# Loops kept on the engines instead of written out, in a two-layer attention and expert kernel

## The chip, the cores and the metric

The kernel runs on one core of one Trainium2 chip. The metric is the device time of one execution in microseconds (us). Three executions of the kernel before took 1290.54, 1291.73 and 1295.01 us, a median of 1291.73 us.

A core has five instruction streams that run beside each other and meet only in semaphores: PE (TensorE, matmuls; a page lists its weight loads as PEld), DVE (VectorE), ACT (ScalarE), POOL (GpSimd) and SP (SyncE, which here only issues DMAs). Each stream is read by a sequencer, which waits for semaphores, works on registers, branches, and hands the other instructions to its engine.

## The reference

Input are tokens x (4 batches, 512 tokens, 256 values), a context of the same shape and a mask. Four blocks follow, each added to x; 16 heads of width 16 throughout. Cut to what matters:

```python
x = x + xattn0(layernorm(x), ctx, ctx, mask)   # masked cross attention
x = x + ffn0(layernorm(x))                     # self attention, then 8 experts (256->1024->256), one per token
x = x + xattn1(layernorm(x), ctx, ctx)         # cross attention with biases
x = x + ffn1(layernorm(x))                     # softmax gate of width 256, 8 experts (256->256), one per token

# attention, for every batch and head
scores = q @ k.T / sqrt(16); weights = softmax(scores); out = (weights @ v) @ W_O
# experts
idx = argmax(gate(x)); y = relu(x @ w1[e] + b1[e]) @ w2[e] + b2[e] for e = idx
```

## The kernel before

The program has five stages of one shape, called in this order on every engine: attention `xa0` (masked), attention `sa0`, experts `me0`, attention `xa1`, experts `me1`. Every engine has a stream of its own, written in the order in which it runs; there is no scheduler. Semaphores carry counts that only grow: `Signal.at(i, k)` gives the count `i * per + lead + k` to wait for in round i.

**Projection** (`project_vector`, `project_gpsimd`, `project_scalar`, `project_tensor`, `project_sync`). Per batch: layer norm statistics on DVE (L423, L426), the reciprocal root on POOL (L529, L531), the normalised tokens on DVE (L435), transposes and q, k, v matmuls on PE (L643, L651, L668, L681), q and k split into three bfloat16 parts (ACT L598 and L603, DVE L454, POOL L536), and the parts stored in HBM by SP (L729). `each_batch` (DVE, POOL) goes over batches 0 to 2 and then does batch 3 apart; `each_pair` (PE, ACT) does batches 0 and 1, then 2 and 3 apart.

**Attention** (`attend_*`). A batch has 4 groups of 4 heads, a group has 16 units of 128 x 512 scores. PE computes, for every unit, transposed scores (L994, with a mask matmul L998 in `xa0`), and the plain scores of a unit 28 ahead (L981), of which DVE takes row maxima (L372 in `xa0`, L376 elsewhere). ACT exponentiates (L908). After every fourth unit PE multiplies by the values (L1008, four float32 matmuls). Three PSUM banks each go round for the two kinds of scores, so PE can be at most three units ahead of ACT and of DVE. SP brings the rows of a group from HBM two groups ahead (`load_stacks`, L334) and puts 12 rows of maxima beside them (L815). `body(b, first, last)` is one batch: it is called for batch 0, for batches 1 and 2 in a loop, and for batch 3.

**Experts** (`gate_*`, `route_*`, `expert_*`, `combine_*`). Tokens are gated (DVE L1336 to L1349), sorted into 23 slots of 128 rows, gathered by POOL (L1595), multiplied slot by slot on PE (L1730, L1738, L1755 in `me0`, L1749 in `me1`, transposes L1721), finished by DVE (L1694) and stored. The expert of a slot is known at run time only: it is loaded into a register, and addresses are worked out from it, so the kernel before has register instructions in these stages. `each_slot` does slots 0 to 5, then two rounds of 6 in a loop, then the last 5.

In the kernel before all of these loops are Python's: each iteration is written into the stream, and every wait compares with a constant.

Of the kernel before, what the change touches and what calls it, by code (L numbers as in the profile page):

```python
# [38 lines left out]
T = S // P  # L39
# [20 lines left out]
class Signal:  # L60
# [6 lines left out]
    def at(self, i, k=0):  # L67

        return i * self.per + (self.lead + k)


# [148 lines left out]
class Attention:  # L220


    def __init__(self, nc, stage, mem, dram, name, w, cross, norms, affine, cols, rows, masked, self_block,
# [8 lines left out]
        def sig(what, per, lead=0):  # L232
            self.used.append(stage.enter_context(nc.semaphore(f"{name}_{what}")))
            return Signal(self.used[-1], per, lead)

        self.stat = [sig(f"stat{n}", T) for n in range(norms)]
        self.aggr = [sig(f"aggr{n}", T) for n in range(norms)]
# [56 lines left out]
def each_batch(eng, body):  # L294

    for b in range(B - 1):
        body(b, b + 1)
    body(B - 1, None)


def each_pair(eng, body):

    for i in range(B // 2 - 1):
        for odd in range(2):
            body(2 * i + odd, 2 * i + (odd + 1), odd)
    for odd in range(2):
        b = B - 2 + odd
        body(b, b + 1 if b + 1 < B else None, odd)
# [56 lines left out]
def maximum(dve, a, G, v, bank):  # L365

    mem = a.mem
    h, t = v // T, v % T
    out = mem.m[:, t, h:h + 1]
    if a.masked:  # L370
        dve.wait_ge(a.s_ps.sem, a.s_ps.at(G, v + 1))
        ins = dve.tensor_tensor_reduce(mem.junk[bank], mem.ps[:, bank, :], mem.mbS[:, t, :], 1.0, FLOOR,  # L372
                                       ALU.add, ALU.max, out)
    else:
        dve.wait_ge(a.s_ps.sem, a.s_ps.at(G, v + 1))
        ins = dve.tensor_reduce(out, mem.ps[:, bank, :], AX.X, ALU.max)  # L376
    ins.then_inc(a.s_max.sem, 1)
# [15 lines left out]
def project_vector(dve, a):  # L393
# [16 lines left out]
    def normalise_first(b):  # L410
        dve.wait_ge(a.scale[0].sem, a.scale[0].at(b, 2))
        if type(b) is not int or b:
            dve.wait_ge(a.hT_ps.sem, a.hT_ps.at(b))
        for t in range(T):
            dve.tensor_scalar(mem.hn[:, t, :], mem.x[:, b, t, :], mem.mv_in[:, b, t, 0:1], mem.rstd_in[:, b, t:t + 1],
                              ALU.subtract, ALU.mult).then_inc(a.first_norm.sem, 1)

    def statistics(b):
        for t in range(T):
            if a.norms == 2:  # L420
                dve.wait_ge(a.first_norm.sem, a.first_norm.at(b, t + 1))
            src = mem.x[:, b, t, :] if a.norms == 1 else mem.hn[:, t, :]
            dve.bn_stats(mem.stats[:, t, :], src).then_inc(a.stat[last].sem, 1)  # L423
        for t in range(T):
            dve.wait_ge(a.stat[last].sem, a.stat[last].at(b, t + 1))
            dve.bn_aggr(mem.mv[:, t, :], mem.stats[:, t, :]).then_inc(a.aggr[last].sem, 1)  # L426

    def normalise(b):

        dve.wait_ge(a.scale[last].sem, a.scale[last].at(b, 2))  # L430
        if a.norms == 1 and (type(b) is not int or b):
# [83 lines left out]
def project_gpsimd(pool, a):  # L515
# [192 lines left out]
def project_sync(sp, a):  # L708
# [98 lines left out]
def attend_sync(sp, a, meanwhile, then=None):  # L807
# [39 lines left out]
    body(0, True, False)  # L847
    for b in range(1, B - 1):
        body(b, False, False)
# [7 lines left out]
def last_sums(eng, a, name, b, k):  # L857
# [13 lines left out]
    eng.tensor_tensor(mem.total_x[:, two, :], x, u, ALU.add).then_inc(a.acc_ready.sem, 1)  # L871
    eng.wait_ge(a.acc_ready.sem, a.acc_ready.at(b, k + 1))
    eng.tensor_copy(x, u).then_inc(a.x_done.sem, 1)


def attend_gpsimd(pool, a):
    mem = a.mem

    def gather(b, g):

        G = NG * b + g
        if not (type(b) is int and G < 2):
            pool.wait_ge(a.pv.sem, a.pv.at(G - 1))
        pool.tensor_copy(mem.vg[g % 2][:, :, :, 0:DK],  # L884
# [5 lines left out]
    for g in range(NG):  # L890
        gather(0, g)
    for b in range(1, B):
        for g in range(NG):
# [5 lines left out]
def attend_scalar(act, a, meanwhile):  # L899
# [56 lines left out]
    body(0, True, False)  # L956
    for b in range(1, B - 1):
        body(b, False, False)
# [7 lines left out]
def attend_tensor(pe, a, meanwhile):  # L966
# [154 lines left out]
    body(0, True, False)  # L1121
    for b in range(1, B - 1):
        body(b, False, False)
# [12 lines left out]
def attend_vector(dve, a, meanwhile, beside=None):  # L1136
# [33 lines left out]
    def block_input(b, k):  # L1170

        u, row = mem.block_in[:, 2 * k:2 * k + 2, :], mem.rows[:, a.rows + 1:a.rows + 2, :].to_broadcast([P, 2, D])
        if type(b) is not int or b:
            dve.wait_ge(a.x_done.sem, a.x_done.at(b - 1, k + 1))
        for t in range(2 * k, 2 * k + 2):
# [45 lines left out]
    body(0, True, False)  # L1221
    for b in range(1, B - 1):
        body(b, False, False)
# [21 lines left out]
class Mixture:  # L1245
# [5 lines left out]
    def __init__(self, nc, stage, mem, dram, name, affine, gate_width, row, hidden, b2, weights, loads,  # L1251
                 x_done, space, acc_stored, gathered, earlier, scattered=None, fetched=None, out_stored=None):
        self.mem, self.dram, self.name, self.affine = mem, dram, name, affine
# [5 lines left out]
        def sig(what, per, lead=0):  # L1259
            self.used.append(stage.enter_context(nc.semaphore(f"{name}_{what}")))  # L1260
            return Signal(self.used[-1], per, lead)

        self.stat = sig("stat", T)
# [40 lines left out]
        if hidden is None:  # L1304
            self.out_stored = Signal(out_stored, 16)


def gate_vector(dve, m):
# [20 lines left out]
    def body(b):  # L1329
# [18 lines left out]
        dve.wait_ge(m.choice.sem, m.choice.at(b, CHOICE - 1))  # L1348
        dve.tensor_copy(mem.expert[:, b, :], mem.expert_u[:, :]).then_inc(m.choice.sem, 1)  # L1349
# [17 lines left out]
    def rest_of_batches():  # L1367
# [3 lines left out]
        for b in range(early, B):  # L1371
            normalise(b)
        for b in range(1, B):
            body(b)
# [213 lines left out]
def expert_gpsimd(pool, m, done=()):  # L1588
# [14 lines left out]
    for stage in done:  # L1603
        for sem in stage.used:
            pool.sem_clear(sem)
# [252 lines left out]
def program(nc, x, ctx_in, mask, wa, wb, wc, cols, rows, b1c, b2, gate0, w1, w2, gate1, we, be, out):  # L1858
# [10 lines left out]
    with ExitStack() as ctx:  # L1869
        mem = Memory(nc, ctx)  # L1870
        def semaphore(name):
            return ctx.enter_context(nc.semaphore(name))

        x_first, x_rest, weights_a, weights_qo, loaded, setup, acc_stored, out_stored = (semaphore(n) for n in (
            "x_first", "x_rest", "weights_a", "weights_qo", "loaded", "setup", "acc_stored", "out_stored"))
        weights = [semaphore(f"weights{i}") for i in range(2)]
# [63 lines left out]
        with ExitStack() as again:  # L1940
# [10 lines left out]
        me1 = Mixture(nc, ctx, mem, dram, "me1", None, D, 4, None, mem.be, (weights[1], 16 * (C * E + NG)), (),  # L1951
                      xa1.x_done, None, None, gathered, 1, fetched=fetched, out_stored=out_stored)

# [159 lines left out]
```

## Time and profile before

| what | value |
|---|---|
| the profiled execution | 1290.54 us |
| its span, first to last instruction | 1288.8 us |
| PE busy | 1142.8 us (89%) |
| DVE, ACT, POOL busy | 851.6, 669.7, 225.5 us |
| mean granted clock of TensorE | 0.945 of full |
| instructions fetched (queues named instruction) | 49 packets of 16 KB, 42 of 8 KB |

The profile shows one execution. Busy time counts an engine's instructions from start to end; register, branch and semaphore instructions are not in it. A row of idle time names the work that ended it. TensorE's clock is granted at one of two levels, 2.4 GHz (1.00) or 1.2 GHz (0.50); a number between them is a mean over a stretch. Time is from the first instruction.

### The profile page before, as it was taken

How to read it: one execution, taken by the hardware profiler on the slowest of the kernel's cores; microseconds unless marked ns; L12 is line 12 of the kernel's file. 1: busy time of each engine (PE TensorE's matmuls, PEld its weight loads, DVE VectorE, ACT ScalarE, POOL GpSimd, SP SyncE). 2: the span in 40 equal slices, each digit the busy share in tenths (PEclk: the TensorE clock that was granted, in tenths of full speed). 3: DMA queues.
4: the chain of work that ended last, by engine and by line, in shares of the span. 5: the costliest groups of instructions: out<-in, count | busy, mean ns of one | idle time of the engine just before them, and what ended most of it. 6: DMA issues, size and time to landing. Idle time of an engine off the chain costs nothing. (4 is left out here: it accounts for less than half of the span.)

```text
span 1288.8 us, 17972 instructions
## 1 busy us (share of the span) xinstructions
PE 1142.8 (89%) x5757; PEld 551.3 (43%) x5786; DVE 851.6 (66%) x2112; ACT 669.7 (52%) x1357; POOL 225.5 (17%) x280
## 2 busy tenths in 40 slices
PE   7989999999988999999968999994989999998490
PEld 4523343433354223333364666663532343335370
DVE  5787777777468888888771222224788888876722
ACT  2446666666633577677712333331536777675350
POOL 5310000000134000000202222213420000101054
PEclk9979999999999899999968999998989999999785
DMA  6943232321038443543291140103773422211064
GB/s 213 314 137 106 79 83 50 84 50 26 1 117 287 122 105 84 130 101 92 71 371 37 31 156 31 32 5 99 249 249 76 103 59 75 71 34 58 25 165 145
DMA packets 103371, 139.32 MB, mean 108 GB/s; under 512 B 8044, under 2 KB 86320, under 8 KB 101872
## 3 DMA queue, kind: packets, MB, share of 16 engines
q1 hardware_dynamic: 99200, 127.94, 33.0%
q0 software_dynamic: 4080, 10.23, 3.0%
q8 instruction: 49, 0.80, 0.3%
q14 instruction: 42, 0.34, 0.1%
HBM read 86.30 MB, written 52.17 MB: 107 GB/s over the span
## 5 line engine op out<-in xcount | busy, mean ns | idle before, releaser
L908 ACT ACTIVATE r<-ps 128x512 f32<-128x512 f32 x768 | 427.7, 599 | 213.0 <-PE ps L994 123.6
L376 DVE TENSOR_REDUCE m<-ps 128x1 f32<-128x512 f32 x512 | 321.1, 683 | 46.9 <-PE ps L981 46.6
L981 PE MATMUL ps<-r 96*128 96x512 bf16 x720 | 281.9, 394 | 20.5 <-DVE m L376 7.0
L994 PE MATMUL ps<-r 99*128 99x512 bf16 x768 | 294.2, 388 | 5.6 <-ACT r L908 5.6
L372 DVE CUSTOM_DVE_ANT_0 r<-ps,r 128x512 bf16<-128x512 f32 x256 | 170.2, 690 | 60.0 <-PE ps L981 59.5
L1008 PE MATMUL ps<-r 128*32 128x512 f32 x1536 | 205.4, 607 | 4.9 <-ACT r L908 3.3
L994 PEld LDWEIGHTS ps<-r 99*128 99x128 bf16 x768 | 74.4, 98 | 212.2 <-ACT r L908 157.4
L981 PEld LDWEIGHTS ps<-r 96*128 96x128 bf16 x720 | 71.3, 99 | 106.8 <-DVE m L376 24.7
L884 POOL COPY r<-r 128x256 f32<-128x256 f32 x48 | 19.0, 399 | 543.6 <-PE ps L1008 543.6
L681 PE MATMUL ps<-r,w 128*128 128x512 f32 x192 | 91.7, 611 | 0.0
L1683 DVE COPY r<-ps 128x512 f32<-128x512 f32 x46 | 31.8, 692 | 90.5 <-PE ps L1730 90.5
L1642 ACT ACTIVATE r<-ps,cols 128x128 f32<-128x128 f32 x46 | 18.6, 454 | 137.7 <-PE ps L1721 137.7
L1730 PE MATMUL ps<-r 128*128 x184 | 86.2, 612 | 2.7 <-issue 0.4
L998 PE MATMUL ps<-r,identb 128*128 128x512 bf16 x227 | 87.2, 384 | 0.0
L1755 PE MATMUL ps<-r 128*128 x368 | 83.3, 379 | 1.1 <-ACT r L1652 1.1
L1694 DVE TENSOR_TENSOR r<-ps,r 128x256 f32<-128x256 f32 x46 | 19.5, 424 | 97.2 <-PE ps L1755 68.8
L598 ACT ACTIVATE r<-ps,cols 128x512 bf16<-128x512 f32 x48 | 32.9, 686 | 94.2 <-PE ps L681 94.2
L1755 PEld LDWEIGHTS ps<-r 128*128 128x128 f32 x368 | 69.8, 190 | 20.2 <-issue 11.9
L536 POOL TENSOR_TENSOR r<-r 128x512 bf16<-128x512 f32 x48 | 55.0, 1163 | 65.6 <-ACT r L603 65.6
L1008 PEld LDWEIGHTS ps<-r 128*32 128x32 f32 x1536 | 30.3, 108 | 84.3 <-ACT r L908 66.6
L1595 POOL DMA_INDIRECT r<-token_rows,source x46 | 44.5, 968 | 69.1 <-DVE source L1534 31.8
L1652 ACT ACTIVATE r<-ps,b1c 128x128 f32<-128x128 f32 x184 | 50.1, 383 | 11.3 <-PE ps L1738 11.2
(155 smaller groups left out, 1274.5 us busy)
## 6 DMA issues: line engine op xcount, KB each, us to landing
r<-q_parts SPq DMA_DIRECT2D x48, 384.0 KB, 5.1
r<-k_parts SPq DMA_DIRECT2D x48, 384.0 KB, 5.9
k_parts<-r SPq DMA_DIRECT2D x24, 384.0 KB, 3.1
q_parts<-r SPq DMA_DIRECT2D x24, 384.0 KB, 3.1
r<-in_w SPq DMA_DIRECT2D x16, 512.0 KB, 4.8
r<-in_w SPq DMA_DIRECT2D x8, 1024.0 KB, 14.5
k_parts<-r SPq DMA_DIRECT2D x24, 256.0 KB, 3.2
q_parts<-r SPq DMA_DIRECT2D x24, 256.0 KB, 3.1
```

What stands on the lines that cost most here:

```text
L372: ins = dve.tensor_tensor_reduce(mem.junk[bank], mem.ps[:, bank, :], mem.mbS[:, t, :], 1.0, FLOOR, ALU.add, ALU.max, out)
L376: ins = dve.tensor_reduce(out, mem.ps[:, bank, :], AX.X, ALU.max)
L536: pool.tensor_tensor(mem.parts[n][:, 2, :], mem.res[n % 2], mem.parts[n][:, 1, :], ALU.subtract).then_inc(a.lo.sem, 1)
L681: ins = pe.matmul(ps[:, QK_BANK + n, :], a.w[:, 0 if of_query(n) else 1, c, (n % C) * P:(n % C + 1) * P], src[:, c, :], start=(c == 0), st ...
L908: act.activation(mem.probs[:, u // HG, u % HG, :], ps[:, ST + (UNITS * g + u) % DEEP, :], ACT.Exp, scale=SCALE).then_inc(a.p_exp.sem, 1)
L981: pe.matmul(ps[:, led_bank(n), :], mem.qst[g][0:ROWS, h, t * P:(t + 1) * P], mem.kst[g][0:ROWS, h, :], start=True, stop=True).then_inc(a.s ...
L994: ins = pe.matmul(out, mem.kst[g][0:KROWS, h, kt * P:(kt + 1) * P], mem.qst[g][0:KROWS, h, :], start=True, stop=not a.masked)
L998: ins = pe.matmul(out, mem.identb[:, :], mem.mbT[:, batch, kt, :].rearrange("p b n -> p (b n)"), start=False, stop=True)
L1008: ins = pe.matmul(ps[h * VW:(h + 1) * VW, OB, :], mem.vg[g % 2][:, kt, h, :], mem.probs[:, kt, h, :], start=(kt == 0), stop=(kt == T - 1))
L1652: ins = act.activation(mem.midT[:, f, :], ps[:, TM[f // 4], (f % 4) * P:(f % 4 + 1) * P], ACT.Relu, bias=mem.b1c[:, bass.ds(e * FT + f, 1)])
L1730: ins = pe.matmul(ps[:, UP[k], :], mem.xT[j % 2][:, c, :], w, start=(c == 0), stop=(c == C - 1))
L1755: ins = pe.matmul(ps[:, DOWN[j % 2], 0:D], mem.midT[:, f, :], w, start=(f == 0), stop=(f == FT - 1))
```

## The change

Seven loops are now loops of the engine that runs them: `Fori(first, end)` emits the body once, sets a register, and ends the body with an addition and a conditional branch back. All five engines have them. The batch number b in the body is then a register. A wait for `Signal.at(b, k)` compares with a register that has to be worked out first, and an address that holds b (of x, v, the mask, rows in HBM) too. Some instructions take no wait on a register; for these `wait_alone` emits a semaphore instruction of its own, which holds the wait and counts up a semaphore that nobody reads. It is written in at ten places, whether b is a register there or not. The semaphore for stored outputs is now made by the stage that uses it, and POOL clears the three new semaphores of the first two stages.

```diff
+def wait_alone(eng, sem, value, passed):
+
+    eng.wait_ge(sem, value)
+    eng.sem_inc(passed, 1)
@@ each_batch
-    for b in range(B - 1):
+    with eng.Fori(0, B - 1) as b:
         body(b, b + 1)
@@ each_pair
-    for i in range(B // 2 - 1):
+    with eng.Fori(0, B // 2 - 1) as i:
@@ maximum, masked
-        dve.wait_ge(a.s_ps.sem, a.s_ps.at(G, v + 1))
+        wait_alone(dve, a.s_ps.sem, a.s_ps.at(G, v + 1), a.passed["dve"])
@@ statistics, normalise
-            dve.wait_ge(a.stat[last].sem, a.stat[last].at(b, t + 1))
+            wait_alone(dve, a.stat[last].sem, a.stat[last].at(b, t + 1), a.passed["dve"])
-        dve.wait_ge(a.scale[last].sem, a.scale[last].at(b, 2))
+        wait_alone(dve, a.scale[last].sem, a.scale[last].at(b, 2), a.passed["dve"])
@@ project_gpsimd
-        pool.wait_ge(a.aggr[last].sem, a.aggr[last].at(b, T))
+        wait_alone(pool, a.aggr[last].sem, a.aggr[last].at(b, T), a.passed["pool"])
@@ project_sync
-        for b in range(0, B - 2):
+        with sp.Fori(0, B - 2) as b:
@@ attend_sync, attend_scalar, attend_tensor, attend_vector: the same in each
-    for b in range(1, B - 1):
+    with sp.Fori(1, B - 1) as b:
         body(b, False, False)
@@ attend_gpsimd
-    for b in range(1, B):
+    with pool.Fori(1, B) as b:
@@ gate_vector
-            dve.wait_ge(m.logit.sem, m.logit.at(b, t // 2 + 1))
+            wait_alone(dve, m.logit.sem, m.logit.at(b, t // 2 + 1), m.passed["dve"])
-            dve.wait_ge(m.choice.sem, m.choice.at(b, t + 1))
+            wait_alone(dve, m.choice.sem, m.choice.at(b, t + 1), m.passed["dve"])
-        for b in range(1, B):
+        with dve.Fori(1, B) as b:
             body(b)
@@ each_slot
-    for i in range(1, rounds):
+    with eng.Fori(1, rounds) as i:
         for j in range(DEPTH):
             body(i * DEPTH + j, j, i)
```

No work on the engines changes its order. What moves is what stands between. First PE, in a group of `sa0`, batch 1: before, around the transposes of the maxima and the first products that follow.

```order
L994 MATMUL ps<-r 128x512
L981 MATMUL ps<-r 128x512
L1016 MATMUL ps<-identb,mparts 12x128 x4
L994 MATMUL ps<-r 128x512
L981 MATMUL ps<-r 128x512
L1008 MATMUL ps<-r 32x512 x4
```

The same place now (L996 and L1002 are the old L994, L989 the old L981, L1024 the old L1016, L1016 the old L1008; an ISA row without a tile is several register operations in one instruction):

```order
L996 REGISTER_ALU
L1002 MATMUL ps<-r 128x512
L988 REGISTER_ALU
L989 MATMUL ps<-r 128x512
L1021 ISA
L1024 MATMUL ps<-identb,mparts 12x128 x4
L996 REGISTER_ALU
L1002 MATMUL ps<-r 128x512
L988 REGISTER_ALU
L989 MATMUL ps<-r 128x512
L1011 REGISTER_ALU
L1016 MATMUL ps<-r 32x512 x4
```

Each of the two matmuls of a unit has a register instruction ahead of it, and so has each set of transposes or products. In the whole loop body of PE these are 157 instructions in `xa0` and 150 in `sa0` and `xa1`, where the body has some 1000 and 832 instructions with weight loads and both passes of float32 matmuls counted.

Second DVE, in the projection of `xa0`, one batch of the loop. Before:

```order
L454 SCALAR_TENSOR_TENSOR r<-ps,cols,r 128x512
L423 BN_STATS stats<-x 128x6 x4
L426 BN_AGGR mv<-stats 128x2 x4
L454 SCALAR_TENSOR_TENSOR r<-ps,cols,r 128x512
L435 TENSOR_SCALAR r<-x,mv,rstd 128x256 x4
```

Now, from the last statistics on (L431 is the old L423, L434 the old L426, L462 the old L454, L443 the old L435). The semaphore instructions of `wait_alone` are not printed in this listing; one stands ahead of each BN_AGGR and ahead of the first L443:

```order
L431 BN_STATS stats<-x 128x6
L74 ISA
L434 BN_AGGR mv<-stats 128x2
L74 REGISTER_ALU
L434 BN_AGGR mv<-stats 128x2
L74 REGISTER_ALU
L434 BN_AGGR mv<-stats 128x2
L460 REGISTER_ALU
L461 REGISTER_ALU
L462 SCALAR_TENSOR_TENSOR r<-ps,cols,r 128x512
L74 ISA
L443 TENSOR_SCALAR r<-x,mv,rstd 128x256 x4
```

Four aggregations that stood in a row are now three instructions each: a register instruction, a semaphore instruction and the aggregation. The DVE body of a batch has 22 or 23 register instructions, and 28 to 30 with semaphore and branch instructions.

## Rows read from the trace of the kernel before

**Rows 1.** The page: busy time, share of the span and instructions.

```profile
PE 1142.8 (89%) x5757; PEld 551.3 (43%) x5786; DVE 851.6 (66%) x2112; ACT 669.7 (52%) x1357; POOL 225.5 (17%) x280
```

**Rows 2.** Windows: length, busy time (instructions) per engine, granted clock, DMA share, GB/s.

```profile
88.00:370.00 282.00, 274.43 (x1528) 110.99 (x1555) 200.82 (x650) 173.33 (x305) 13.67 (x27) 1.00 0.21 55
441.00:656.00 215.00, 203.77 (x1196) 78.75 (x1195) 183.35 (x413) 149.14 (x282) 21.57 (x34) 1.00 0.42 113
...
893.00:968.00 75.00, 61.19 (x208) 31.75 (x208) 62.84 (x115) 30.30 (x52) 29.47 (x32) 0.84 0.66 214
968.00:1182.00 214.00, 206.98 (x1204) 75.10 (x1204) 173.21 (x369) 152.24 (x292) 16.95 (x26) 1.00 0.26 67
...
1226.00:1258.00 32.00, 29.47 (x134) 22.93 (x134) 9.76 (x23) 16.52 (x44) 17.82 (x19) 0.90 0.62 169
```

**Rows 3.** Waits, whole span: who waited for whom, us, times, longest.

```profile
PEld ps L981 <- DMA r<-k_parts: 10.0, 13, 1.6
PE ps L1721 <- DMA r<-token_rows,source: 10.2, 4, 4.8
```

**Rows 4.** Timeline of PE in `xa1`: start, length, instruction, idle before.

```profile
1072.67 0.39 PE L994 MATMUL ps<-r 99*128 99x512 bf16 x1
1072.90 0.38 PE L981 MATMUL ps<-r 96*128 96x512 bf16 x1
1073.12 0.38 PE L994 MATMUL ps<-r 99*128 99x512 bf16 x1
```

**Rows 5.** Timeline of PE: the routing matmuls of `me0`.

```profile
675.76 1.11 PE L1556 MATMUL ps<-r 128*128 128x69 bf16 x16 [6.88 <-DVE r L1522]
```

**Rows 6.** Chain that ended last, in `me1`: start, us, what (DVEq is DVE's sequencer).

```profile
1237.88 0.07 DVEq L1694
1237.96 0.05 issue
...
1243.54 0.22 PE ps L1721 x2
1243.76 0.87 PE ps L1749 x4
```

**Rows 7.** DMA queues: packets, MB, share of 16 engines; issues: KB, us to landing.

```profile
q8 instruction: 49, 0.80, 0.3%
q14 instruction: 42, 0.34, 0.1%
...
cols<-in_cols SPq DMA_DIRECT2D x1, 10.0 KB, 1.8
```

**Rows 8.** Chain that ended last, in the projection of `xa1`.

```profile
905.45 0.29 DVE mv L426 x3
905.74 0.08 issue
905.82 0.24 POOL var L529
906.05 0.07 issue
906.13 1.05 POOL rstd L531
```

**Rows 9.** Chain that ended last, in the gate of `me1`.

```profile
1193.43 0.18 DVE expert_u L1347
1193.63 0.04 DVE expert L1349
```

**Rows 10.** Timeline of the weight loads in `sa0`, batch 1: waits for a stack.

```profile
537.60 0.10 PEld L981 LDWEIGHTS ps<-r 96*128 96x128 bf16 x1 [0.45 <-DMA r<-k_parts]
550.33 0.10 PEld L981 LDWEIGHTS ps<-r 96*128 96x128 bf16 x1 [0.18 <-DMA r<-k_parts]
564.62 0.10 PEld L981 LDWEIGHTS ps<-r 96*128 96x128 bf16 x1 [0.99 <-DMA r<-k_parts]
```

**Rows 11.** Windows around a fall of the clock, columns as in rows 2.

```profile
60.00:80.00 20.00, 15.07 (x56) 5.81 (x54) 19.04 (x53) 7.46 (x11) 5.26 (x6) 0.89 0.74 266
80.00:100.00 20.00, 19.13 (x78) 6.00 (x80) 14.28 (x47) 9.16 (x16) 0.00 (x0) 0.77 0.36 97
...
380.00:400.00 20.00, 16.91 (x62) 9.80 (x62) 14.17 (x33) 10.69 (x18) 8.71 (x9) 1.00 0.82 244
```

More of the change, by code:

```diff
@@ L234, in sig @@
             return Signal(self.used[-1], per, lead)
+        self.passed = {eng: stage.enter_context(nc.semaphore(f"{name}_{eng}_passed")) for eng in ("dve", "pool")}
         self.stat = [sig(f"stat{n}", T) for n in range(norms)]
@@ L410, in normalise_first @@
     def normalise_first(b):
-        dve.wait_ge(a.scale[0].sem, a.scale[0].at(b, 2))
+        wait_alone(dve, a.scale[0].sem, a.scale[0].at(b, 2), a.passed["dve"])
         if type(b) is not int or b:
@@ L871, in last_sums @@
     eng.tensor_tensor(mem.total_x[:, two, :], x, u, ALU.add).then_inc(a.acc_ready.sem, 1)
-    eng.wait_ge(a.acc_ready.sem, a.acc_ready.at(b, k + 1))
+    wait_alone(eng, a.acc_ready.sem, a.acc_ready.at(b, k + 1), a.passed[name])
     eng.tensor_copy(x, u).then_inc(a.x_done.sem, 1)
@@ L882, in gather @@
         if not (type(b) is int and G < 2):
-            pool.wait_ge(a.pv.sem, a.pv.at(G - 1))
+            wait_alone(pool, a.pv.sem, a.pv.at(G - 1), a.passed["pool"])
         pool.tensor_copy(mem.vg[g % 2][:, :, :, 0:DK],
@@ L956, in attend_scalar @@
     body(0, True, False)
-    for b in range(1, B - 1):
+    with act.Fori(1, B - 1) as b:
         body(b, False, False)
@@ L1121, in attend_tensor @@
     body(0, True, False)
-    for b in range(1, B - 1):
+    with pe.Fori(1, B - 1) as b:
         body(b, False, False)
@@ L1173, in block_input @@
         if type(b) is not int or b:
-            dve.wait_ge(a.x_done.sem, a.x_done.at(b - 1, k + 1))
+            wait_alone(dve, a.x_done.sem, a.x_done.at(b - 1, k + 1), a.passed["dve"])
         for t in range(2 * k, 2 * k + 2):
@@ L1221, in attend_vector @@
     body(0, True, False)
-    for b in range(1, B - 1):
+    with dve.Fori(1, B - 1) as b:
         body(b, False, False)
@@ L1251, in __init__ @@
     def __init__(self, nc, stage, mem, dram, name, affine, gate_width, row, hidden, b2, weights, loads,
-                 x_done, space, acc_stored, gathered, earlier, scattered=None, fetched=None, out_stored=None):
+                 x_done, space, acc_stored, gathered, earlier, scattered=None, fetched=None):
         self.mem, self.dram, self.name, self.affine = mem, dram, name, affine
@@ L1261, in sig @@
             return Signal(self.used[-1], per, lead)
+        self.passed = {eng: stage.enter_context(nc.semaphore(f"{name}_{eng}_passed")) for eng in ("dve",)}
         self.stat = sig("stat", T)
@@ L1304, in __init__ @@
         if hidden is None:
-            self.out_stored = Signal(out_stored, 16)
+            self.out_stored = sig("out_stored", 16)
 def gate_vector(dve, m):
@@ L1347, in body @@
         dve.tensor_scalar(mem.expert_u[:, :], mem.idx8[:, :, 0], E - 1, None, ALU.bitwise_and).then_inc(m.choice.sem, 1)
-        dve.wait_ge(m.choice.sem, m.choice.at(b, CHOICE - 1))
+        wait_alone(dve, m.choice.sem, m.choice.at(b, CHOICE - 1), m.passed["dve"])
         dve.tensor_copy(mem.expert[:, b, :], mem.expert_u[:, :]).then_inc(m.choice.sem, 1)
@@ L1603, in expert_gpsimd @@
     for stage in done:
-        for sem in stage.used:
+        for sem in (*stage.used, *stage.passed.values()):
             pool.sem_clear(sem)
@@ L1872, in semaphore @@
             return ctx.enter_context(nc.semaphore(name))
-        x_first, x_rest, weights_a, weights_qo, loaded, setup, acc_stored, out_stored = (semaphore(n) for n in (
-            "x_first", "x_rest", "weights_a", "weights_qo", "loaded", "setup", "acc_stored", "out_stored"))
+        x_first, x_rest, weights_a, weights_qo, loaded, setup, acc_stored = (semaphore(n) for n in (
+            "x_first", "x_rest", "weights_a", "weights_qo", "loaded", "setup", "acc_stored"))
         weights = [semaphore(f"weights{i}") for i in range(2)]
@@ L1951, in program @@
         me1 = Mixture(nc, ctx, mem, dram, "me1", None, D, 4, None, mem.be, (weights[1], 16 * (C * E + NG)), (),
-                      xa1.x_done, None, None, gathered, 1, fetched=fetched, out_stored=out_stored)
+                      xa1.x_done, None, None, gathered, 1, fetched=fetched)
         with nc.Block() as block:
```

## The prediction

> **What bounds the kernel now.** I read the page's busy line first: PE is busy 89% of the span, the next engine 66% [rows 1]. Then windows cut at the stages. In the three attention loops PE is busy 274.43 of 282, 203.77 of 215 and 206.98 of 214 us at clock 1.00, 685.18 of 711 us together, 55% of the span; the projection of `xa1` has 61.19 of 75 us with DVE at 62.84 [rows 2]. So two kinds of stretch have to be told apart. In attention an added instruction costs nothing while PE's sequencer stays ahead of its engine, and a stop of PE costs its whole length. In projection and gate DVE and POOL are links of the chain of waits [rows 8, 9], and instructions between short operations count.
>
> The change takes no engine work away and adds none. Every term is a sequencer's: register instructions, semaphore instructions, branches, and the fetching of instructions after a branch back.
>
> **What a register instruction costs.** The nearest row: in `me1` the chain passes DVE's sequencer, where such an instruction takes 0.07 us and 0.05 us pass before the operation behind it starts [rows 6]. So 0.07 us where instructions queue, up to 0.12 us where one stands between a wait and its operation. For PE there is a bound. A slot of `me1` takes 0.22 + 0.87 = 1.09 us, just its matmuls at full rate [rows 6], although its stream already has about 8 register, load and wait instructions beside 16 weight loads and matmuls. Sixteen pairs of load and matmul of 69 columns go by in 1.11 us, 0.069 us a pair at most [rows 5]. So the 8 take at most (1.09 - 8 x 0.069) / 8 = 0.067 us each.
>
> **Attention bodies: 0.** A unit of `sa0` or `xa1` has two matmuls, 0.23 and 0.22 us apart [rows 4]: 0.45 us. Its sequencer work after the change is 2 x 0.069 for the pairs and 2 x 0.07 for the registers, 0.28 us; with 0.12 us a register it is 0.38 us. Both stay under 0.45 us, and `xa0` has a third matmul per unit. ACT and DVE have one register instruction per 0.6 us operation. What hides the cost is PE's own matmul time; without it the 157 + 2 x 150 register instructions of PE's bodies, run twice, would be 914 x 0.07 = 64 us, which is the far end.
>
> **Branches back in attention: 7.2.** Each body runs twice, so each engine goes back once per attention. After a branch the instructions have to be there. They are streamed: PE's packets are 0.80 MB / 49 = 16 KB, 256 instructions, the others' 8 KB, 128 instructions [rows 7]. PE's bodies are 1000, 832 and 832 instructions, 3.9, 3.3 and 3.3 packets. If the start of the body is gone, PE stands until it has come again. The queue's 0.3% of 16 engines' 1288.8 us over 49 packets is 1.26 us a packet, and the smallest load has a landing time of 1.8 us for 10 KB [rows 7]: at most 1.8 + 1.3 = 3.1 us, at least the 0.12 us of the branch if the start is still there. I take 2.4 us, nearer to the fetch. ACT, DVE and SP go back at the same unit, and their stops lie beside PE's, so one stop counts per loop: 3 x 2.4 = 7.2 us (0.4 to 9.3).
>
> By the Trainium skill (Runtime: NRT & Kernel Launch, Instruction fetch mechanics) a taken branch whose target is not among the two pages held forces a fetch before execution goes on, and prefetch runs forward only; by that rule all three branches stop PE, as in the term taken. The same section gives PE room for 2048 instructions; a body of 1000 would fit, and if all of that room counted the term would fall to its low end, 0.4 us. It gives 16 KiB for every engine's block, where this trace has 8 KB for the others.
>
> **Branches back over slots: 3.6.** One per engine in `me0` and in `me1`. PE's body in `me0` is 669 instructions, 2.6 packets, in a stretch that PE bounds: 2.4 us. In `me1` (151 instructions) the gathers leave PE waiting at times [rows 3], so half, 1.2 us. Bounds 0.2 and 6.2 us.
>
> **Projection: 4.5.** `each_batch` runs its body three times in each of three stages, nine in all. The chain goes from statistics through aggregations (three in 0.29 us, 0.10 us each) to POOL and the root [rows 8], then to the tokens and PE. An aggregation is now three instructions of the sequencer, at least 0.21 us: four of them add 0.5 us, the wait on its own ahead of POOL's first operation and of the tokens 0.12 us each, POOL's register instructions and the addresses of the statistics the rest: 1.0 us. Nine times 1.0 is the top. These stretches are partly held by DMAs (share 0.66 on average, and 0.82 in one stretch with POOL and DVE half free [rows 2, 11]), which such a delay lies beside. I take half, 4.5 us (1 to 9).
>
> **Gate: 2.7.** Three looped batches in each of two stages. Five operations in a row depend on the one before; two of them are 0.20 us apart and 0.17 us long [rows 9]. Each gets a register instruction or a wait of its own: 5 x 0.09 = 0.45 us, six times 2.7 us (1 to 4).
>
> **SP: 2.0.** Per group four or five register instructions come in ahead of the loads, 0.5 us. In `sa0`, batch 1, the score matmuls already wait for their stack by 0.45, 0.18 and 0.99 us [rows 10], so the room there is nil and 4 x 0.5 = 2.0 us go through. Elsewhere PE waits 13 times in the whole span, mostly in batch 0 [rows 3], which isn't looped. No row shows a load whose HBM address is a register; if it costs SP nothing more the term is 2.0, and at another 0.5 us for each of two loads in 8 groups it is 10.
>
> **Small branches: 1.5.** About ten that lie on the chain, of DVE in projection and gate, with bodies of 34 to 54 instructions, which I take to be still at hand: 0.15 us each. If half of them found theirs gone it would be 5 x 1.8 = 9.
>
> **The sum.** 0 + 7.2 + 3.6 + 4.5 + 2.7 + 2.0 + 1.5 = 21.5 us. On the profiled execution, 1290.54 us (span 1288.8), that is 1312.0 us; the median of the runs shown is 1.2 us above it, so 1313 us. The cases at the low ends of all terms give 0.4 + 0.2 + 1 + 1 + 2 + 0.5 = 5 us.
>
> **Rivals.** *Nothing is refetched, 1300 us.* The bodies are still there at every branch back, and only the register instructions of projection, gate and SP remain: 4.5 + 2.7 + 2.0 + ten branches at 0.15, less than 11 us with the range, 1298 to 1303. For it speaks that 3.9 packets are little, against it that the fetches are as many as the stream has packets [rows 7], one after another, with nothing that shows a store of old ones.
>
> *The clock falls more often, 1330 us.* TensorE was at 1.00 over 20 us in which PE was busy 16.91 us, and went down to half behind a stretch with 15.07 of 20 [rows 11]. A projection whose batches are a microsecond longer has a lower share. One more period of half clock per projection, as long as the one whose mark is the mean 0.77 (9 of 20 us and what lies before it, some 14 us), costs up to half its length, 7 us; three are 20 us. [...]
>
> *PE's sequencer becomes the bound in attention, 1340 us.* If a wait against a register costs 0.15 us more than one against a constant, a unit needs 0.58 us instead of 0.45 in `sa0` and `xa1`; two looped batches of 64 units in each are 256 x 0.13 = 33 us, less what products (1 us per four units) win back. The bound of 0.067 us above speaks against it, but that stretch waits against constants.
>
> *Not slower, 1292 us.* The place is the projection. If each of them is held by its DMAs and not by DVE, its nine delays vanish, SP's vanish where a stack has room, and with the bodies still at hand the whole change is what is left of the gate, about 1 to 3 us. It decides at a term under 4 us in all. DMA shares of 0.66 to 0.82 speak for it, the chain through DVE and POOL [rows 8] against it. A gain would need a fetch that is saved; PE's idle time in attention is only 26 of 711 us [rows 2], mostly waits for others, so a gain over 4 us has next to no room.
>
> **How the numbers follow.** The measurement can tell about 0.3%, 3.9 us, from no change. Forecast (1303 to 1324): 0.56. Nothing refetched (1296 to 1303): 0.16. Clock or sequencer (above 1324): 0.16. Not slower: 0.12, of which faster 0.03. So faster 0.03, same 0.09, slower 0.88. The range for 8 in 10 leaves out the not-slower case and the far half of the slow ones: 1296 to 1335 us. The likeliest case alone has 1303 to 1324.
>
> **What would show it.** In the profile after: near the middle of each attention PE should have one gap of 2 to 3 us that ends in "issue", and the instruction queues more packets than 49 and 42. PE's matmuls in a looped batch should be as far apart as in a written one (0.22 us). The projections should be 1 to 3 us longer, with aggregations 0.2 us apart; the waits for k_parts in `sa0`, batch 1, longer by half a microsecond. The forecast is wrong if the packets stay at 91 without gaps (then the first rival), if the looped batches are longer throughout (the third), or if the mean clock falls below 0.93 (the second).

## The result, and the profile after

The changed kernel took 1304.7 us (median of 4, 1301.71 to 1306.56), the kernel before 1292.44 us (1290.54 to 1295.01) beside it. The ratio is 1.0079, 95% interval 1.0056 to 1.0101: slower by 10.2 us (7 to 13). A second set gave 1.0083 (1.0067 to 1.0099), 10.7 us. I had forecast 1313 us, +21.3: the direction was right, the size twice what came, and the time lies in the lower part of the range.

The profiled execution spans 1303.4 us from first to last instruction, 14.6 us more than the 1288.8 before, so some 4 us of what this one profile shows are not in the difference of the runs. First the page: busy times as in [rows 1], and the queues that bring instructions, as in [rows 7].

```profile
PE 1144.9 (88%) x5786; PEld 550.4 (42%) x5787; DVE 855.6 (66%) x2113; ACT 669.1 (51%) x1358; POOL 225.5 (17%) x280
...
q8 instruction: 40, 0.66, 0.2%
q14 instruction: 46, 0.38, 0.1%
```

The engines are as busy as before, within 4 us each; the whole growth is time between instructions. PE fetched 9 packets fewer, the others 4 more. The records hold 12524 different instructions of PE before and 10281 now (an iteration counted once), 48.9 and 40.2 packets of 256, and 49 and 40 were fetched: PE fetched nothing twice. That alone speaks against my largest term. The others hold 5372 different instructions, 42.0 packets of 128, and fetched 46: some of theirs came twice.

Windows over the same stretches as in [rows 2], shifted by as much as PE's stream had moved (length, busy time of PE, PEld, DVE, ACT, POOL, clock, DMA share, GB/s):

```profile
88.00:370.00 282.00, 275.57 (x1552) 110.36 (x1551) 200.69 (x649) 171.45 (x302) 13.34 (x26) 1.00 0.21 55
445.00:660.00 215.00, 202.80 (x1192) 78.75 (x1193) 182.27 (x410) 147.51 (x280) 21.46 (x33) 1.00 0.41 113
...
900.00:976.00 76.00, 60.28 (x208) 31.44 (x208) 62.59 (x113) 30.17 (x52) 29.36 (x32) 0.86 0.65 211
976.00:1190.00 214.00, 206.82 (x1208) 75.92 (x1208) 174.63 (x372) 152.19 (x292) 16.94 (x26) 1.00 0.26 68
```

In attention PE's busy time per window is within 1.2 us of before. The waits as in [rows 3]: those for a stack are shorter than before, not longer.

```profile
PE ps L1731 <- DMA r<-token_rows,source: 10.1, 3, 4.9
PEld ps L989 <- DMA r<-k_parts: 7.5, 8, 1.4
```

The timeline of PE at the place of [rows 4] (start, length, instruction). The matmuls of a looped batch are 0.22 us apart, as written out:

```profile
1072.67 0.39 PE L1002 MATMUL ps<-r 99*128 99x512 bf16 x1
1072.89 0.38 PE L989 MATMUL ps<-r 96*128 96x512 bf16 x1
1073.11 0.38 PE L1002 MATMUL ps<-r 99*128 99x512 bf16 x1
```

And PE where it goes back in `sa0` (the branch is at 536.0). I had put a stop of 2.4 us of PE here; there is none:

```profile
535.27 0.38 PE L989 MATMUL ps<-r 96*128 96x512 bf16 x1
535.58 1.06 PE L1016 MATMUL ps<-r 128*32 128x512 f32 x8
536.58 0.39 PE L1002 MATMUL ps<-r 99*128 99x512 bf16 x1
536.80 0.38 PE L989 MATMUL ps<-r 96*128 96x512 bf16 x1
```

One engine does stop. DVE goes back in `xa0` at 219.26, and the first instruction of its body comes 2.86 us later, with two packets for the smaller streams (at 220.3 and 222.8) meanwhile. Its timeline there:

```profile
219.12 0.69 DVE L380 CUSTOM_DVE_ANT_0 r<-ps,r 128x512 bf16<-128x512 f32 x1
219.73 0.08 DVE L380 DVE_READ_ACCUMULATOR2_ANT m<- 128x1 f32 x1
222.42 0.69 DVE L380 CUSTOM_DVE_ANT_0 r<-ps,r 128x512 bf16<-128x512 f32 x1 [2.60 <-issue]
```

PE was far enough ahead: its matmuls at 222 are 0.22 us apart, and between 220 and 240 it loses 0.1 us against before.

To see where the 10 us are I took the time between the same two weight loads of PE in each trace (they come in the same order). What grew, in us, in two profiles of the changed kernel (the second is e5's):

| stretch | before | after, first | after, second |
|---|---|---|---|
| projection of `sa0` | 58.2 | +2.05 | +2.02 |
| projection of `xa1` | 71.3 | +1.44 | +0.72 |
| looped batches of `xa0`, `sa0`, `xa1` | 137.8, 112.2, 108.9 | +0.31, +1.46, +0.20 | +0.28, +1.22, +0.19 |
| gate of `me0`, of `me1` | 16.8, 25.1 | +1.39, +1.52 | +1.81, +1.52 |
| looped slots of `me0`, of `me1` | 100.2, 17.6 | +1.23, +0.57 | +1.31, +0.14 |
| `me1`, slots 0 to 5 | 9.4 | +3.89 | -0.48 |

The growth sits in short chains: projection, gate, slots. The looped batches of attention, 359 us, add 2.0 and 1.7 us, nearly all of it in `sa0` (see e12).

### The profile page after: what moved, and what is told of

The parts are those of the page before. It is cut to its first block, busy times and chain, and to the rows that moved or that the text cites. A ratio compares the mean times of both kernels' runs of the same rounds, so it can differ in the third digit from the quotient of the medians.

```text
span 1303.4 us, 21372 instructions
## 1 busy us (share of the span) xinstructions
PE 1144.9 (88%) x5786; PEld 550.4 (42%) x5787; DVE 855.6 (66%) x2113; ACT 669.1 (51%) x1358; POOL 225.5 (17%) x280
## 4 chain that ended last, share of the span: by engine, by line
PE 67%; DVE 12%; DMA 7%; issue 6%; ACT 4%; POOL 2%; SPq 1%; DVEq 1%; POOLq 0%; ACTq 0%
PE ps L1016 12%; PE ps L1002 11%; PE ps L989 9%; PE ps L1740 7%; PE ps L1765 6%; DMA r<-k_parts 5%; PE ps L1006 4%; PE ps L1067 3%; DVE m L384 2%; PE ps L676 2%; PE ps L1759 2%; ACT r L916 2%; PE ps L689 2%; PE ps L1748 1%; DVE r L443 1%
## 5 line engine op out<-in xcount | busy, mean ns | idle before, releaser
L1002 PE MATMUL ps<-r 99*128 99x512 bf16 x768 | 293.9, 388 | 6.2 <-ACT r L916 6.2
L989 PE MATMUL ps<-r 96*128 96x512 bf16 x720 | 281.7, 393 | 19.1 <-DVE m L384 7.0
L1016 PE MATMUL ps<-r 128*32 128x512 f32 x1536 | 204.5, 604 | 5.5 <-ACT r L916 4.5
L1002 PEld LDWEIGHTS ps<-r 99*128 99x128 bf16 x768 | 74.4, 98 | 211.7 <-ACT r L916 152.2
L989 PEld LDWEIGHTS ps<-r 96*128 96x128 bf16 x720 | 71.2, 99 | 107.8 <-DVE m L384 24.2
L892 POOL COPY r<-r 128x256 f32 (+1 forms) x48 | 19.0, 400 | 543.7 <-PE ps L1016 543.7
L1006 PE MATMUL ps<-r,identb 128*128 128x512 bf16 (+1 forms) x256 | 98.2, 384 | 0.0
L1016 PEld LDWEIGHTS ps<-r 128*32 128x32 f32 x1536 | 30.3, 107 | 84.1 <-ACT r L916 63.0
## 6 DMA issues: line engine op xcount, KB each, us to landing
r<-in_w SPq DMA_DIRECT2D x8, 1024.0 KB, 14.6
```

What stands on the lines that cost most here:

```text
L989: pe.matmul(ps[:, led_bank(n), :], mem.qst[g][0:ROWS, h, t * P:(t + 1) * P], mem.kst[g][0:ROWS, h, :], start=True, stop=True).then_inc(a.s ...
L1002: ins = pe.matmul(out, mem.kst[g][0:KROWS, h, kt * P:(kt + 1) * P], mem.qst[g][0:KROWS, h, :], start=True, stop=not a.masked)
L1006: ins = pe.matmul(out, mem.identb[:, :], mem.mbT[:, batch, kt, :].rearrange("p b n -> p (b n)"), start=False, stop=True)
L1016: ins = pe.matmul(ps[h * VW:(h + 1) * VW, OB, :], mem.vg[g % 2][:, kt, h, :], mem.probs[:, kt, h, :], start=(kt == 0), stop=(kt == T - 1))
```

## The experiments

Theory A, formed from this: the branches back are free, because PE still holds the body; what costs is the loops' register instructions and, once e1 had run, any instruction put between a wait and its operation. Its rival is my prediction's: refetching.

### Attention loops alone: e2 and e7

Of the changed kernel only the attention loops stay; in e7 `wait_alone` also leaves out its counting instruction where the value is a constant, so that the operation itself waits, as before.

```diff
 # each_batch, each_pair, project_sync, gate, each_slot:
-    with eng.Fori(0, B - 1) as b:
+    for b in range(0, B - 1):
 # e7 alone, wait_alone:
     eng.wait_ge(sem, value)
-    eng.sem_inc(passed, 1)
+    if type(value) is not int:
+        eng.sem_inc(passed, 1)
```

> Only the loops of the three attentions are loops of the engines (all five engines); projection, gate and slots are written out. The traces show PE's stream 0.6 us later at the end of xa0, level through xa1, and no fetch of PE for 80 us in the second iteration. Theory A (PE holds its body, nothing is refetched): 1293 to 1296 us, 1 to 3 us over before. Rival, that each of the three branches back stops PE for 2.4 us as I had predicted: 1299 to 1301 us.

> Only the attention loops are loops of the engines, and a separate wait is written only where its value is a register; everywhere else the operation waits itself, as in the kernel before. Theory A (attention is free, as PE holds its body): 1290 to 1293 us, within 0.2% of before. Rival (a branch back costs 2.4 us each): 1297 us.

e2: 1297.37 us, ratio 1.0071 (1.0044 to 1.0098), but its runs scatter over 11 us. e7: 1290.03 against 1290.78 us, ratio 0.9993 (0.9982 to 1.0004), with 42 packets for PE instead of 49. So the attention loops alone cost at most 0.5 us; e2 contains the separate waits besides, which turned out to be a cost (e1).

One thing differs between the two. DVE's body in `xa0` has 325 instructions in all of these kernels. In e2 and in both profiles of the changed kernel it was not held: from the branch to the next instruction 2.88, 2.86 and 2.83 us. In e7 it was, 0.35 us, and the others' packets are 42 there against 50 in e2. The body stands at another place in DVE's stream (it begins near instruction 330 in e7, 399 and 436 in the changed kernel and e2); that the place decides is not shown. So e7 does not contain this stop. What it costs is small: `xa0`'s looped batches are 0.1 us longer in the changed kernel than in e7, and up to 0.9 us longer in e2.

### How long a body PE holds: e13, e14, e9a, e9b

As e7, with counting instructions put into the looped body of `sa0` on PE: 9, 13, 17 and 26 per unit in e13, e14, e9a and e9b. They change no data. Each of these kernels ran once.

```diff
             for u in range(UNITS):
+                for _ in range(17 if a.name == "sa0" and not first and not last else 0):
+                    pe.sem_inc(a.passed["pe"], 1)
                 transposed_scores(b, g, u, first)
```

> As e7 (only the attention loops looped, waits joined), with 17 counting instructions more per unit on PE in the looped body of sa0: 832 + 64 x 17 = 1920 instructions, 7.5 packets of 16 KB. They change no data. Theory A (PE holds what it has run, up to 2048 instructions, as the Trainium skill has it: Runtime: NRT & Kernel Launch, Instruction fetch mechanics): the second iteration fetches nothing, and PE goes back within 0.3 us. Theory B (what is held is about the 1000 instructions seen so far): 7 or 8 packets again in the second iteration, and one stop of 1 to 3 us at the branch back. In both the two looped batches are longer by 2 x 64 x (17 x 0.05 us - what a unit's matmuls hide): some 50 to 70 us in all.

> The same with 26 instructions per unit: 832 + 64 x 26 = 2496 instructions, 9.75 packets. Theory A (room for 2048): the start is gone at the branch back, the second iteration fetches its 9 or 10 packets again and PE stops there once, for a packet's 1 to 3 us, the price that my prediction put on each branch back. Theory C (the room is larger): no fetch in the second iteration and no stop.

> As e9a with 9 counting instructions per unit: a body of 832 + 576 = 1408 instructions, 5.5 packets. A body of 1000 was held, one of 1920 not. If the room is 2048 less what is fetched ahead of need, this one is held: no stop at the branch back (under 0.4 us) and no fetches for most of the second iteration. If the room is about 1024: a stop of 3.5 us and 6 more packets.

> The same with 13 per unit: 832 + 832 = 1664 instructions, 6.5 packets. Held or not closes the gap between 1408 and 1920; with a room of 2048 and one packet ahead it is held, with half of that not.

The recorded body of `sa0` has 784 instructions, 48 fewer than the 832 that I had counted (and `xa0`'s about 955, not 1000); the table has the recorded numbers.

| kernel | body | PE's packets | from the branch to PE's next instruction | time |
|---|---|---|---|---|
| e7 | 784 | 42 | 0.29 us | 1290 us |
| e13 | 1360 | 44 | 0.28 us | 1396 us |
| e14 | 1616 | 45 | 0.28 us | 1478 us |
| e9a | 1872 | 55 | 3.70 us | 1554 us |
| e9b | 2448 | 61 | 3.48 us | 1737 us |

The added instructions themselves are 2.3, 3.3, 4.3 and 6.5 packets. So e13 and e14 have what the longer text explains (44, 45), and e9a has 9 more than the 46 it explains: it fetched its body of 7.3 packets again. e9b, with a body of 9.6, has 12 to 13 more. Why both are 2 or 3 above their body is not shown. PE around the branch in e9a, timeline; the idle time before the first matmul of the units beside it is 1.8 to 1.9 us, at the branch 5.75:

```profile
661.04 0.61 PE L1003 MATMUL ps<-r 99*128 99x512 bf16 x1 [1.81 <-issue]
661.44 0.63 PE L990 MATMUL ps<-r 96*128 96x512 bf16 x1
667.82 0.61 PE L1003 MATMUL ps<-r 99*128 99x512 bf16 x1 [5.75 <-issue]
668.22 0.63 PE L990 MATMUL ps<-r 96*128 96x512 bf16 x1
670.77 0.60 PE L1003 MATMUL ps<-r 99*128 99x512 bf16 x1 [1.92 <-issue]
```

The same place in e14, body still held (the first row shown is the unit before the branch, the third the one after it):

```profile
623.52 0.39 PE L1003 MATMUL ps<-r 99*128 99x512 bf16 x1 [0.63 <-ACT r L917]
623.74 0.38 PE L990 MATMUL ps<-r 96*128 96x512 bf16 x1
626.27 0.61 PE L1003 MATMUL ps<-r 99*128 99x512 bf16 x1 [2.15 <-issue]
626.67 0.63 PE L990 MATMUL ps<-r 96*128 96x512 bf16 x1
628.49 0.61 PE L1003 MATMUL ps<-r 99*128 99x512 bf16 x1 [1.19 <-ACT r L917]
```

So a refetch costs PE more than I had priced: 3.5 to 3.7 us, above my upper bound of 3.1. It isn't paid up to 1616 instructions. By the Trainium skill (Runtime: NRT & Kernel Launch, Instruction fetch mechanics) PE has room for 2048 instructions; 1616 held and 1872 not agrees with that room less a block of 256 that is already being filled ahead, which is an estimate of mine. The same section's two-page window, by which all these bodies would be refetched, doesn't hold for PE here. The expectation of "50 to 70 us" for the added work was far off; see the last section.

### The separate waits: e1 and e6

e1 is the changed kernel with all loops written out: only `wait_alone` is left of the change, at eleven places (three of them, in attention, are not in the shortened diff above). e6 is the same, with its two instructions in the other order, so that the count goes first and the operation itself waits.

```diff
 # e6, wait_alone:
-    eng.wait_ge(sem, value)
-    eng.sem_inc(passed, 1)
+    eng.sem_inc(passed, 1)
+    eng.wait_ge(sem, value)
```

> All loops are written out again, as in the kernel before; only the separate semaphore instructions of wait_alone are left. Theory A (what costs is the loops: their register instructions and what happens around branches): within 0.1% of the kernel before, 1291 to 1294 us, since a semaphore instruction takes 0.02 to 0.05 us in the trace and about 8 of them per batch of a projection or gate lie on the chain: 18 batches x at most 0.1 us = 2 us. Theory B (the separate waits are what makes projection and gate longer): 1297 us or more, half of the 12 us.

> As e1, all loops written out, but the counting instruction of wait_alone stands ahead of the wait, so that the operation itself waits, as in the kernel before: the same number of instructions, another place of the wait. Theory A (what costs is the step from a separate wait to its operation, 0.11 to 0.14 us where operations depend on one another): 1290 to 1292 us, and statistics to root again 1.76 us, root to tokens 1.38 us, gate 1.40 us in me0. Rival (any further instruction in these chains costs, wherever it stands): as e1, 1295 to 1297 us, with 1.92, 1.50 and 1.97 us.

e1: 1295.87 us, ratio 1.0043 (1.0027 to 1.0059), +5.5 us: half of the whole change, and against theory A as I then had it. e6: 1292.82 us, ratio 1.0014 (1.0005 to 1.0024), +1.8 us. The last two operations of a gate show it. In e1 (timeline of DVE, `me0`) the second starts 0.31 us after the first:

```profile
667.61 0.17 DVE L1357 TENSOR_SCALAR expert_u<-idx 128x4 uint32<-128x4 uint32 x1
667.92 0.17 DVE L1359 CAST expert<-expert_u 128x4 f32<-128x4 uint32 x1
```

In e6 it is 0.20 us, as before [rows 9], although the counting instruction is there too:

```profile
665.58 0.17 DVE L1357 TENSOR_SCALAR expert_u<-idx 128x4 uint32<-128x4 uint32 x1
665.78 0.17 DVE L1359 CAST expert<-expert_u 128x4 f32<-128x4 uint32 x1
```

Not all of the cost goes with the order: a gate batch of `me0` stays 0.36 us longer than before, of 0.57 in e1, and one of `me1` 0.05 us. Four of each are 1.6 us, about e6's whole 1.8. So there the further instruction costs wherever it stands, as the rival had it; in the projection the order decides.

And the chain of e1 in a projection, to be held against [rows 8] (POOLq and DVEq are sequencers, L75 the counting instruction):

```profile
936.84 0.03 issue
936.87 0.02 POOLq L75
936.88 0.14 issue
937.02 0.24 POOL var L537
937.26 0.07 issue
937.34 1.05 POOL rstd L539
938.38 0.03 issue
938.41 0.02 DVEq L75
938.43 0.09 issue
938.52 1.04 DVE r L443
```

Before, 0.08 us lay between the aggregation and POOL's operation; in e1 it is 0.18 us, and 0.14 instead of 0.03 us between the root and DVE. Measured in all kernels, in us (typical batch; a projection from the first statistics to POOL's first operation, from there to the tokens; a gate from the start of the last sum of logits to the end of the last operation):

| | statistics to root | root to tokens | gate `me0` | gate `me1` |
|---|---|---|---|---|
| before, e7, e8, e12 | 1.76 | 1.38 | 1.40 | 4.19 |
| e6, count first | 1.76 | 1.38 | 1.76 | 4.24 |
| e1, all written out | 1.92 | 1.50 | 1.97 | 4.35 |
| after, looped batches | 1.92 | 1.50 to 1.87 | 2.53 | 4.51 |

The wait and its operation being two instructions costs 0.10 to 0.11 us per link of a chain. It is paid in each of the 12 projected and 8 gated batches, looped or not: 12 x (0.16 + 0.12) + 4 x 0.57 + 4 x 0.16 = 6.3 us, if all of it lies on the path that ends last; e1's 5.5 (3.5 to 7.6) agrees with that.

### Projection and gate loops: e4

e4 keeps of the changed kernel the loops of projection and gate, on all engines, and the separate waits.

> Only projection (DVE, POOL, PE, ACT, SP) and gate are loops of the engines. Theory A: 3 projections at about 1.3 us and two gates at 0.8 and 1.6 us as the shift of PE's stream shows them, 6 us in all: 1297 to 1300 us. My prediction's terms for the same part were 4.5 + 2.7 us. Rival (the chain of DMAs hides it): within 2 us of before.

1299.47 us, ratio 1.0074 (1.0058 to 1.009). Less the waits of e1 that is 0.31%, 4 us, for the loops, with 0.16% of uncertainty on either ratio. The last two rows of the table give 3 x 0.56 + 3 x 0.16 = 2.2 us for the gates, the tokens of `sa0` and the rest of its projection about 1; the rest is within the uncertainty. DVE at the end of a looped gate, in the changed kernel: 0.42 us from one operation to the next, where a register instruction and the counting instruction stand between.

```profile
668.16 0.17 DVE L1357 TENSOR_SCALAR expert_u<-idx 128x4 uint32<-128x4 uint32 x1
668.58 0.17 DVE L1359 CAST expert<-expert_u 128x4 uint32 x1 [0.24 <-DVE expert_u L1357]
```

### Slot loops: e3, e8, e10, e11

e3 keeps of the changed kernel the slot loops and the separate waits, e8 the slot loops alone; e10 loops over slots on PE only, e11 on ACT, DVE and SP only.

```diff
-def each_slot(eng, body):
+def each_slot(eng, body, looped):
...
+    if looped:
         with eng.Fori(1, rounds) as i:
             for j in range(DEPTH):
                 body(i * DEPTH + j, j, i)
+    else:
+        for i in range(1, rounds):
+            for j in range(DEPTH):
+                body(i * DEPTH + j, j, i)
 # e10; e11 has them the other way round
-    each_slot(pe, body)
+    each_slot(pe, body, True)
-    each_slot(dve, body)
+    each_slot(dve, body, False)
```

> Only the loops over slots are loops of the engines. In the traces this stage has the largest growth: me1 from the first gather to the last store is 5.5 us longer, me0 1 us. Theory A (the looped slots cause it, by register instructions and branches in me1's short slots): 1297 to 1300 us, and the stall of ACT of 2.1 us ahead of the fifth slot is there again. Rival (the stall lies before the loop, in instructions that are the same in both kernels, and comes from where the stream's blocks happen to begin, so it is not the loop's): 1293 to 1296 us, and the stall is gone or elsewhere.

> Only the slot loops are loops of the engines, with the waits of the rest as in the kernel before. Theory A: me0's loop 1.3 us longer and me1's 1.2 to 1.9 us, as in e3 and the changed kernel: 1292.5 to 1294.5 us. Rival (e3 was slower by the separate waits alone and the loops are hidden): 1290 to 1291.5 us.

> As e8, but only PE's slot loops are loops of the engine; ACT, DVE and SP have theirs written out. Theory A (PE is the bound in me0, so its register instructions in front of waits are what costs): me0's 12 looped slots 1.2 to 1.4 us longer as in e8, me1's about 0.5. Rival (the others' delays): me0's loop within 0.2 us of before. Whole kernel 1292 to 1294 us by A, 1291 by the rival.

> The complement of e10: ACT, DVE and SP loop over slots, PE has them written out. Theory A: me0's loop within 0.2 us of before, as ACT and DVE have time there; me1's loop 0.5 to 1 us longer, since there DVE and ACT are links of the chain slot by slot. Rival: me0's loop 1.2 us longer here.

e3: 1299.46 us, 1.0071 (1.0054 to 1.0089). Less e1 that is 0.28%. e8: 1294.52 us, 1.0028 (1.0017 to 1.0038), the same without the waits. e10: 1293.98 us, 1.0030 (1.0018 to 1.0042). e11: 1291.49 us, 1.0007 (0.9991 to 1.0023). The looped slots of `me0` are 1.35, 1.22 and 0.10 us longer in e8, e10 and e11. So in `me0` it is PE's own register instructions, 0.1 us for each of 12 slots: PE's idle time before the first matmul of a slot is 0.11 us before and 0.21 us now, and where one register instruction stood ahead of it there are two, 0.10 us apart. The changed kernel's waits show them one by one, where before the shorter gap made no such row (who waited for whom: us, times, longest):

```profile
PE ps L1740 <- ACT r L1652: 2.6, 12, 0.2
```

The same wait in e10, with its lines 6 further on:

```profile
PE ps L1746 <- ACT r L1658: 3.0, 13, 0.4
```

And in e11, PE written out:

```profile
PE ps L1746 <- ACT r L1658: 0.2, 1, 0.2
```

The wait is put down to ACT, which had ended; what stands between ACT's end and the matmul is PE's register instruction for the value to wait for. In `me1` the looped slots are 0.75 and 0.79 us longer in e8 and e10 and 0.41 us shorter in e11. That leaves some 1.5 of e8's 3.6 us outside the looped slots, and no run here shows where from.

### SP's loops: e12

```diff
 # each_batch, each_pair, gate, each_slot, and attention on PE, ACT, DVE, POOL
-    with eng.Fori(...) as b:
+    for b in range(...):
```

> Only SP's loops in projection and attention are loops of the engine; every other engine has its stream written out, waits joined. My prediction put 2.0 us on SP, for register instructions ahead of the loads of a group: then 1292.5 to 1293 us, and sa0's batches 1 and 2 about 2 us longer. Rival (loads are issued early enough, the change costs nothing): within 0.1% of before, and batches 1 and 2 of sa0 within 0.5 us.

1295.89 against 1296.75 us, ratio 1.0000 (0.9983 to 1.0017); `sa0`'s batches 1 and 2 are 0.70 us longer, between the 2 us of my term and the 0.5 us of the rival. So SP's loops cost less than I had put, but the whole time tells nothing finer than 2.2 us, and whether the 0.70 us are theirs is open. That stretch is 1.2 to 1.5 us longer in the changed kernel, 1.25 in e6 without any loop, and -0.05 in e7; what moves it stays open.

### The changed kernel again: e5

> The changed kernel itself, as the measure for the others of this set and for a second profile. From e1 to e4 the parts add up to 5.5 (separate waits) + 1.5 (attention) + 3.6 (slots) + 3.6 (projection, gate) = 14 us over before if nothing overlaps: 1302 to 1305 us. Theory A: the profiles repeat the stage times within 0.3 us in the gates and projections. Open: the first six slots of me1, 3.9 us longer in the first profile with ACT standing for 2.1 us ahead of the fifth slot. If it belongs to the program it comes again at the same slot; if it was scatter of one execution it is gone.

1300.54 us, ratio 1.0083 (1.0067 to 1.0099). Most stage times came again (table above; the projection of `xa1` and the gate of `me0` differ by 0.7 and 0.4 us, more than the 0.3 that I had expected), but not the 3.9 us of `me1`'s first slots. In the first profile ACT turned slot 4 late (timeline of ACT); the records have its wait over at 1240.5, with the operation 2.1 us behind:

```profile
1239.27 0.42 ACT L1674 ACTIVATE r<-r 128x256 f32<-128x256 f32 x1
1242.68 0.38 ACT L1647 ACTIVATE r<-ps 128x256 f32<-128x256 f32 x1 [3.00 <-DMA r<-k_parts]
```

In e5 no such gap is there, and in e12, where ACT's stream has no loop, it is:

```profile
1230.10 0.41 ACT L1675 ACTIVATE r<-r 128x256 f32<-128x256 f32 x1
1233.33 0.38 ACT L1648 ACTIVATE r<-ps 128x256 f32<-128x256 f32 x1 [2.83 <-PE ps L1732]
```

So it needs no loop on ACT and does not come in every execution of the changed kernel; what causes it is open. One profile alone would have given the wrong largest term.

## Why the prediction was wrong in size, step by step

- **What bounds the kernel, and attention bodies: 0.** Right, also in the reason: 0.22 us between matmuls, and e7 at 0.9993. My counts of PE's looped bodies were some 5% high in attention (784 and about 955 recorded) and more in the slots (549 and 127, not 669 and 151); nothing turned on it.
- **Branches back in attention: 7.2.** This is the step that failed. The term held that PE's body is gone at the branch back. Its price was too low (3.5 to 3.7 us where a body is not held), its condition wrong: I read "a packet per 256 instructions, one after another" as "nothing is kept". Those packets only show that before never went back. On PE 0.27 to 0.29 us pass from the branch to the next instruction, and its weight loads come 0.17 us later for it in `xa0` and 0.00 in `sa0` and `xa1`; the term's low end of 0.4 us, reached if a body of 1000 fits, is near what came. The one body that was fetched again is DVE's in `xa0`. There I had the condition right and the price near (2.86 us), and missed that PE's lead hides all but 0.1 us of it.
- **Branches back over slots: 3.6.** No refetch here either (46 packets in e8, and its 11954 different instructions are 46.7). The slots do cost, 3.6 us in e8 (2.2 to 4.9); that it is my number is luck. In `me0` 1.3 us are 0.1 us of register work per slot on PE, which I had left at nothing; in `me1` up to 0.8; the rest is open.
- **Projection: 4.5.** Size about right, 12 x 0.28 = 3.4 us plus one of the loops, cause half wrong: I charged nine looped batches, and the waits are paid in all twelve.
- **Gate: 2.7.** Mis-sized: 2.9 us of waits in eight batches and 2.2 us of loops in six, 5.1. I counted five links and one batch kind; the four searches for an index each have a separate wait too, and with a register 0.56 us a batch more.
- **SP: 2.0.** At most 0.7 us in `sa0`'s looped batches (e12). I let room of nil at three waits stand for the whole; the waits for a stack shrank from 10.0 to 7.5 us.
- **Small branches: 1.5.** Not seen as a term of their own; apart from the one in `xa0`, DVE goes on 0.08 to 0.5 us after most of its branches.
- **The sum.** Waits 6.3, gate loops 2.2, loops of projection about 1, slots 1.3 in `me0` and 0.1 to 0.8 in `me1`: 10.9 to 11.6 us, against 10.2 and 10.7 measured. Of my 21.5 us, 7.2 + 3.6 were for stops of PE that did not happen, and 2.0 + 1.5 for terms that no run shows at that size.
- **Rivals.** "Nothing is refetched, 1300 us", at 0.16, had the mechanism right as far as PE goes, and I had its argument in hand; of its 10.7 us, the 3.5 of SP and small branches were not seen, and slots and more of the gate came in their place, so that its sum is so near is partly luck. The clock (0.948 after, 0.945 before), PE's sequencer in attention and "not slower" are refuted.

## What to carry to other kernels

Keeping a loop on the engine was free here where the engine had work queued and the body was held (on PE 1616 instructions were, 1872 were not; on DVE 325 were in one kernel and not in another): the attention loops alone leave the time at 0.9993 and fetch fewer instructions. What costs is above all an instruction between a wait and the operation that it releases, 0.1 us a link, so write the separate wait only where the value is a register, and leave short dependent chains (gate, statistics) written out. Before pricing a risk such as a refetch, ask whether a row shows its condition, not only its price.

## What the runs showed of the hardware that I had not expected

- A counting semaphore instruction costs PE far more than its recorded 0.05 us. In `sa0` 1152, 1664, 2176 and 3328 of them made the batches 100, 181, 264 and 443 us longer than before: 0.16 us for each further one, and in e9a one starts 0.15 us after the other. The first few per unit are hidden by matmuls.
- PE's granted clock fell in these kernels too: the mean was 0.853 in e9a and 0.798 in e9b, against 0.947 in e7. There PE stood idle more than 1 us ahead of about 90 and 125 of the 128 units of `sa0`'s looped batches, over which the granted clock was 0.58 and 0.51.
- DVE, with packets of 128 instructions, did not hold a body of 325 in three profiles (a stop of 2.83 to 2.88 us) and held the same body in e7 (0.35 us).
- The wait in an instruction of its own costs 0.10 to 0.11 us, the same two instructions in the other order almost nothing in projection (1.76 and 1.38 us again) and 0.36 us for a whole gate batch of `me0` (1.76 against 1.40).
